# Attention's instruction order comes from a wider search, value sums may wait three tiles, and the last group runs its query blocks in another order

## The chip, the cores and the metric

One core of a Trainium2 chip runs the whole kernel. The metric is the device time of one execution in microseconds (us), as the median of repeated runs.

## What is computed

A cross-attention and a routed feed-forward network, each with a residual. The core of the reference:

```python
qh = (q @ Wq.T + bq).reshape(Bb, Lq, H, hd).transpose(0, 2, 1, 3)      # q = layernorm(x), 4096 x 512, 16 heads of 32
kh = (kv @ Wk.T + bk) ...                                              # kv: 3202 x 512
scores = jnp.einsum('bhqd,bhkd->bhqk', qh, kh) * scale
mask = jnp.arange(Lkv)[None, :] <= jnp.arange(Lq)[:, None]
attn = jax.nn.softmax(jnp.where(mask, scores, -inf), axis=-1)
out = jnp.einsum('bhqk,bhkd->bhqd', attn, vh)
x = x + out @ Wo.T + bo
# feed-forward: x = x + layernorm(W_dec(sigmoid(W_c2s(top-2 of 8 experts(W_s2c(sigmoid(W_enc(layernorm(x)))))))))
```

The attention is causal: a query sees keys up to its own index.

## The kernel before

Four stages follow one another: projections of keys, values and queries (0 to 289 us), attention (289 to 2083 us), the output projection, and the feed-forward network. The change is about attention, and about the order in which the two stages after it go through the rows.

**Tiles.** The 16 heads are taken in 4 groups of 4 heads (`NG`, `HG`). In each group the 4096 queries are 8 blocks of 512 (`QB`, named j = 0 to 7), and the keys are 26 tiles of 128. Block j sees `key_tiles(j)` = 4, 8, 12, 16, 20, 24, 26, 26 key tiles. A step (`ALL_STEPS`) is one group, block and key tile, with four heads. In the last tiles of a block, on the diagonal, only 384, 256 or 128 queries are left.

**Work of a step.** TensorE makes four score matmuls (line 1215, keys by queries) into a ring of three banks, `s_bank`. ScalarE takes the exponentials (line 1046) into one of six slots of `pT`. TensorE weighs the values with them (line 1232), always two steps together, a "pair of tiles". In the program's listing this is 8 matmuls of 512 columns; the profiler records each as two.

**Row maxima.** The softmax maximum is found ahead. For each block TensorE computes the scores a second time, queries by keys (line 1168, one "unit" is 128 queries by up to 512 keys of one head), into a ring of four banks, `m_bank`, and VectorE reduces each (line 1063). When a block's units are done, its maxima are transposed (line 1179) and copied into the rows that scores of that block use.

**Denominators.** The exponentials of a step are summed for the softmax by one of three ways, `adder(j, kt)`: GpSimd adds the tile to `part_sum` (line 986), or a 1 MB DMA issued by GpSimd adds it to one of two `moved_sum` chains (lines 969 and 972), or a matmul against ones takes it from `pT` (line 1200). Block 0 uses a copy on GpSimd (line 984) for its first tile. In the very last block, from key tile 18, VectorE adds instead of GpSimd (line 1113). Two steps into the next block, TensorE sums the parts (lines 1192, 1195, 1200), after it has waited for all adds and both chains.

**A slot of `pT`** is free for step S + 6 when the values of step S have been weighed and its add or transfer is done (`reuse_slot` on ScalarE).

**What sets the order.** Each engine takes its instructions in program order. The order on TensorE is written by a search when the kernel is built (`Orders`). At each point it may place a score, a unit or a pair of values; it holds the states with the least lost TensorE time by its own constants for TensorE, ScalarE and VectorE. Two bounds matter here: a pair of values is forced when 4 scores stand behind its tiles (`VALUES_BEHIND`), and 60 states are kept (`KEPT`). The search knows nothing of the time of GpSimd's adds, of transfers, or of when they free a slot.

Of the kernel before, what the change touches and what calls it, by code (L numbers as in the profile page):

```python
# [9 lines left out]
ALU = mybir.AluOpType  # L10
# [3 lines left out]
P = 128  # L14
# [452 lines left out]
STEPS = [(j, kt) for j in range(QB) for kt in range(key_tiles(j))]  # L467
ST = len(STEPS)
FIRST_STEP = [STEPS.index((j, 0)) for j in range(QB)] + [ST]
ALL_STEPS = [(g, s, j, kt) for g in range(NG) for s, (j, kt) in enumerate(STEPS)]  # L470
assert all(key_tiles(j) % 2 == 0 for j in range(QB))


def query_buffer(g, j):
    return (QB * g + j) % QBUFS


def query_loads(g, j):

    return (QB * g + j) // QBUFS + 1  # L480
# [19 lines left out]
def adder(j, kt):  # L500

    if kt > 4 * j or kt == KT - 1:
        return "matmul"
    return "transfer" if j and kt and kt % 2 == 0 and kt <= key_tiles(j) - 4 else "pool"


def pool_adds(j, kt):

    return adder(j, kt) == "pool" and (kt != 0 or j == 0)
# [23 lines left out]
PO = sum(pool_adds(j, kt) for j, kt in STEPS)  # L533
PO_BEFORE = [sum(pool_adds(j, kt) for j, kt in STEPS[:s]) for s in range(ST + 1)]
TR_BEFORE = [[sum(moves(j, kt, c) for j, kt in STEPS[:s]) for s in range(ST + 1)] for c in range(CHAINS)]
TR = [TR_BEFORE[c][ST] for c in range(CHAINS)]


DEN_AFTER, INVERT, SPREAD, NORMALISE, STORE = 2, 1, 2, 3, 7
SUMS_BEHIND = {ST * g + FIRST_STEP[j + 1] + DEN_AFTER: (g, j) for g in range(NG) for j in range(QB) if (g, j) != (NG - 1, QB - 1)}  # L540

# [16 lines left out]
NU = sum(map(len, UNITS))  # L558
UNITS_BEFORE = [sum(map(len, UNITS[:j])) for j in range(QB + 1)]
# [18 lines left out]
def work_axis():  # L578

    t, at = 0, []  # L580
    for S, (g, s, j, kt) in enumerate(ALL_STEPS):
# [11 lines left out]
def released(at, g, j, c):  # L593
# [1611 lines left out]
```

## Time and profile before

| | us |
|---|---|
| median of 3 runs | 2960.18 (2959.51 to 2963.02) |
| the profiled execution | 2962.7 |
| its span, first to last instruction | 2961.1 |
| TensorE busy | 2870.6 (97%) |
| VectorE busy | 1850.8 (63%) |
| ScalarE busy | 1521.0 (51%) |
| GpSimd busy | 1427.1 (48%) |

The span is the profiled execution less 1.6 us around it. "Busy" of TensorE covers pipelined matmuls, so that 97% is not the share in which it does useful work: what a matmul costs is read from the distance between starts. The mean granted clock of TensorE is 0.98 of full speed.

### The profile page before, as it was taken

The numbers are of one execution on the slowest core, as the hardware profiler recorded it, in microseconds if no ns is written. First come the engines' busy times: TensorE is split into PE (matmuls) and PEld (weight loads), VectorE is DVE, ScalarE is ACT, GpSimd is POOL, SyncE is SP. The second block draws the span as 40 slices with busy tenths as digits, with TensorE's granted clock in tenths as the row PEclk, the third lists the DMA queues.
The fourth block names the chain that finished last, engine by engine and source line by source line (L and its number), as shares of the span: only waits on it lengthen the run. The fifth ranks groups of instructions, "written<-read, shape, count | busy, mean of one in ns | idle before, by whom it ended". The sixth has DMA issues, their size and how long they took to land. (4 is left out here: it accounts for less than half of the span.)

```text
span 2961.1 us, 42860 instructions
## 1 busy us (share of the span) xinstructions
PE 2870.6 (97%) x15944; PEld 1702.9 (58%) x15944; DVE 1850.8 (63%) x3451; ACT 1521.0 (51%) x2896; POOL 1427.1 (48%) x657
## 2 busy tenths in 40 slices
PE   8999999999999999999999999999889999999996
PEld 7877555555555554555554555543675666655664
DVE  4367888886688776688775787851653443344434
ACT  3232455666566666566666566676334433344332
POOL 0000365778565788566788556786841110111110
PEclk9998899999999999999999999999999999999998
DMA  6558456668656778665778555687691111011000
GB/s 236 192 191 248 116 140 150 152 155 194 162 150 149 157 158 200 154 147 140 158 166 203 137 139 119 161 187 177 234 299 54 43 43 40 4 43 43 29 29 15
DMA packets 139750, 408.20 MB, mean 138 GB/s; under 512 B 12672, under 2 KB 29568, under 8 KB 112928
## 3 DMA queue, kind: packets, MB, share of 16 engines
q0 software_dynamic: 32272, 226.77, 32.5%
q1 hardware_dynamic: 102096, 169.34, 19.9%
q10 hardware_dynamic: 5184, 9.44, 1.0%
q8 instruction: 126, 2.06, 0.3%
q14 instruction: 72, 0.59, 0.1%
HBM read 114.59 MB, written 70.78 MB: 63 GB/s over the span
## 5 line engine op out<-in xcount | busy, mean ns | idle before, releaser
L1063 DVE TENSOR_REDUCE row_max<-m_bank 128x1 f32<-128x512 f32 (+4 forms) x2240 | 1253.6, 622 | 267.9 <-PE m_bank L1168 173.1
L1046 ACT ACTIVATE pT<-s_bank 128x512 f32<-128x512 f32 (+5 forms) x2176 | 1086.7, 579 | 648.3 <-PE s_bank L1215 471.5
L986 POOL TENSOR_TENSOR part_sum<-part_sum,pT 128x2048 f32<-128x2048 f32 x192 | 887.8, 4624 | 124.9 <-ACT pT L1046 120.9
L1215 PE MATMUL s_bank<-q_sb,k_sb 104*128 104x512 f32 (+3 forms) x2176 | 839.3, 411 | 12.6 <-ACT pT L1046 8.5
L1168 PE MATMUL m_bank<-k_sb,q_sb 96*128 96x512 f32 (+4 forms) x2240 | 843.0, 410 | 7.5 <-POOL max_terms L958 2.5
L1168 PEld LDWEIGHTS m_bank<-k_sb,q_sb 96*128 96x128 f32 x2240 | 432.5, 196 | 204.9 <-DVE row_max L1063 128.3
L1215 PEld LDWEIGHTS s_bank<-q_sb,k_sb 104*128 104x128 f32 x2176 | 410.5, 192 | 208.8 <-ACT pT L1046 122.5
L1232 PE MATMUL o_bank<-pT,v_sb 128*32 128x512 f32 (+5 forms) x4352 | 498.6, 575 | 0.0
L986 POOL TENSOR_TENSOR part_sum<-pT 128x2048 f32<-128x2048 f32 x28 | 127.7, 4560 | 307.7 <-ACT pT L1046 159.9
L1232 PEld LDWEIGHTS o_bank<-pT,v_sb 128*32 128x32 f32 (+1 forms) x4352 | 113.4, 109 | 229.4 <-ACT pT L1046 115.8
L1640 POOL TENSOR_TENSOR f_var_eps<-f_mean_var,eps 128x4 f32<-128x4 f32 x8 | 1.6, 201 | 484.4 <-DVE f_mean_var L1813 484.4
L1654 ACT ACTIVATE sT<-ring,be_col 128x512 f32<-128x512 f32 x59 | 40.6, 688 | 236.0 <-PE ring L1844 236.0
L972 POOL DMA_DIRECT2D moved_sum<-pT x152 | 137.8, 906 | 28.2 <-ACT pT L1046 17.3
L1090 DVE STREAM_TRANSPOSE den<-m_bank 128x512 f32<-128x512 f32 x32 | 22.9, 716 | 164.5 <-PE m_bank L1200 153.1
L1799 DVE CAST sp_hi<-sp_f 128x512 fp32r<-128x512 f32 x64 | 27.3, 426 | 154.9 <-PE acc L1950 132.3
L1887 PE MATMUL ring<-c_parts,wo_w 64*128 64x512 f32 x768 | 113.6, 416 | 6.0 <-ACT y L1677 3.6
L1844 PE MATMUL ring<-f_x_hi,we_hi 128*128 128x512 f32 x256 | 110.2, 431 | 3.9 <-PEq L1836 3.9
L1950 PE MATMUL acc<-wd_hi,sp_hi 128*128 128x512 f32 x256 | 110.8, 433 | 0.0
L280 POOL TENSOR_TENSOR q_var_eps<-q_mean_var,eps 128x4 f32<-128x4 f32 x8 | 1.6, 199 | 223.0 <-DVE q_mean_var L276 223.0
L1887 PEld LDWEIGHTS ring<-c_parts,wo_w 64*128 64x128 f32 x768 | 68.1, 186 | 62.6 <-ACT raw L1683 23.6
L1844 PE MATMUL ring<-f_x_hi,we_lo 128*128 128x512 f32 x256 | 102.1, 399 | 0.0
L1844 PE MATMUL ring<-f_x_lo,we_hi 128*128 128x512 f32 x256 | 102.1, 399 | 0.0
(195 smaller groups left out, 3479.8 us busy)
## 6 DMA issues: line engine op xcount, KB each, us to landing
moved_sum<-pT POOLq DMA_DIRECT2D x208, 1024.0 KB, 7.4
q_sb<-qT_hi SPq DMA_DIRECT2D x64, 256.0 KB, 5.1
k_sb<-kT_hi SPq DMA_DIRECT2D x48, 256.0 KB, 8.5
x_in<-in_x SPq DMA_DIRECT2D x8, 1024.0 KB, 6.0
qT_hi<-q_hi SPq DMA_DIRECT2D x8, 1024.0 KB, 4.2
qT_lo<-q_lo SPq DMA_DIRECT2D x8, 1024.0 KB, 6.5
q_sb<-qT_lo SPq DMA_DIRECT2D x32, 256.0 KB, 4.6
aT<-o_sb ACTq DMA_DIRECT2D x32, 256.0 KB, 5.2
```

Of the source, the lines that this page charges most:

```text
L972: pool.dma_start(moved_sum[:, c], pT[:, slot(S)], accum_op=ALU.add).then_inc(moved[c], 16)
L986: pool.tensor_tensor(total, pT[:, slot(S - 1), :, q0:] if j and kt == 1 else total, pT[:, slot(S), :, q0:], ALU.add).then_inc(pool_added, 1)
L1046: act.activation(pT[0:rows, slot(S), h, q0:], s_bank[(HG * S + h) % S_RING][0:rows, q0:], ACT.Exp, scale=SCALE).then_inc(exp_done, 1)
L1063: dve.tensor_reduce(row_max[:, j % 2, r, h, c:c + 1], m_bank[p % M_BANKS][:, 0:n], AX_X, ALU.max).then_inc(unit_max, 1)
L1168: mm = pe.matmul(out[:, 0:n], q_sb[query_buffer(g, j)][0:R_MAX, h, r * P:(r + 1) * P], k_sb[0:R_MAX, h, at:at + n], start=True, stop=not m ...
L1215: mm = pe.matmul(out[:, q0:], k_sb[0:R_END, h, at:at + P], q_sb[query_buffer(g, j)][0:R_END, h, q0:], start=True, stop=kt < 4 * j)
L1232: mm = pe.matmul(o_bank[h * HD:(h + 1) * HD, q0:], v_sb[0:rows, kt, h * HD:(h + 1) * HD], pT[0:rows, slot(S), h, q0:], start=kt == 0, stop ...
L1654: act.activation(sT[:, m], src[:, :], ACT.Sigmoid, bias=be_col[:, m:m + 1]).then_inc(ring_free, 1)
L1799: dve.tensor_copy(sp_hi[:, m % 2], sp_f[:, m % 2]).then_inc(sp_hi_ready, 1)
L1844: mm = pe.matmul(dst[:, :], ww[:, c, cols], xx[:, c], start=(c == 0 and k == 0), stop=(c == DC - 1 and k == 2))
L1887: mm = pe.matmul(dst[k][:, :], ww[rows, p, c * P:(c + 1) * P], c_parts[rows, part], start=n == 0, stop=n == 2)
L1950: mm = pe.matmul(acc[k][:, :], a[:, m % 2, rows], ww[:, m], start=(m == 0 and n == 0), stop=(m == FC - 1 and n == 2))
```

## The change

- `VALUES_BEHIND` goes from 4 to 12 scores (three tiles); before a block's denominators it stays 4 (`SUMS_LATE`). `KEPT` goes from 60 to 200.
- The search's state gains GpSimd's time, the ends of the two transfer chains and the time at which each slot comes free (`summed`), with constants for an add, a transfer and the normalising.
- In the last group of heads the blocks are taken as 0, 1, 2, 4, 6, 7, 5, 3 (`LAST_ORDER`). All counters that were worked out from the block's number now go by its place in the order (`NUMBER`, `START`).
- VectorE's adds of the last block (`vector_adds`) are gone; GpSimd or transfers make them. Block 0 takes its first tile by a matmul in place of a copy on GpSimd.
- The output projection and the feed-forward network go through the rows in `LAST_ORDER` too (`block_rows`). The inputs of the output projection are loaded at the start of the last but two and of the last block. GpSimd's part of the feed-forward network is written out for each block, no longer as a loop. `STORE` goes from 7 to 6 steps.

```diff
-STEPS = [(j, kt) for j in range(QB) for kt in range(key_tiles(j))]
...
+LAST_ORDER = (0, 1, 2, 4, 6, 7, 5, 3)
+ORDER = [tuple(range(QB))] * (NG - 1) + [LAST_ORDER]
+BLOCKS = [(g, j) for g in range(NG) for j in ORDER[g]]
...
-    if kt > 4 * j or kt == KT - 1:
+    if j == 0 or kt > 4 * j or kt == KT - 1:
         return "matmul"
-    return "transfer" if j and kt and kt % 2 == 0 and kt <= key_tiles(j) - 4 else "pool"
+    return "transfer" if kt % 2 == 0 and kt and kt <= key_tiles(j) - 4 else "pool"
...
-LAST_ADDS = 18
-
-
-def vector_adds(g, j, kt):
-
-    return (g, j) == (NG - 1, QB - 1) and kt >= LAST_ADDS and pool_adds(j, kt)
...
+T_ADD, T_MOVE_BEGUN, T_MOVE, T_SCALED = 4.75, 1.05, 8.3, 1.3
 T_AHEAD, LATE_COST = 3.0, 0.05
-VALUES_BEHIND, KEPT = 4, 60
+VALUES_BEHIND, SUMS_LATE, KEPT = 12, 4, 200
...
+    def summed(self, x, S, end):
+
+        _, j, kt = ALL_STEPS[S]
+        kind, pool, chains, free = adder(j, kt), x.pool, x.chain_end, 0
+        if kind == "transfer":
+            c = chain(j, kt)
+            pool = max(pool, end, x.sums_end if starts_chain(j, kt) else chains[c]) + T_MOVE_BEGUN
+            free = pool + T_MOVE
+            chains = chains[:c] + (free,) + chains[c + 1:]
+        elif kind == "pool" and kt:
+            pool = free = max(pool, end) + T_ADD
...
-        act = max(x.act, pe + T_TO_READ) + 0.06 + (T_EXP - 0.06) * widths(j, kt)
+        act = max(x.act, pe + T_TO_READ, x.slot_end[0] + T_TO_WRITE if h == 0 else 0) + 0.06 + (T_EXP - 0.06) * widths(j, kt)
...
-        if values_may and x.n >= 2 * HG * (x.v + 1) + VALUES_BEHIND:
+        behind = SUMS_LATE if 2 * (x.v + 1) in SUMS_BEHIND else VALUES_BEHIND
+        if values_may and x.n >= 2 * HG * (x.v + 1) + behind:
             return [self.values(x)]
```

What the search makes of this is seen in the built programs. TensorE in block 7 of the second group, around key tiles 18 to 21, where before stands (s_bank: scores, m_bank: units, o_bank: values):

```order
L1215 MATMUL s_bank<-q_sb,k_sb 128x512 x2
L1232 MATMUL o_bank<-pT,v_sb 32x512 x8
L1215 MATMUL s_bank<-q_sb,k_sb 128x512 x2
L1168 MATMUL m_bank<-k_sb,q_sb 128x512 x2
L1215 MATMUL s_bank<-q_sb,k_sb 128x512
L1168 MATMUL m_bank<-k_sb,q_sb 128x512
L1215 MATMUL s_bank<-q_sb,k_sb 128x512
L1168 MATMUL m_bank<-k_sb,q_sb 128x512
L1215 MATMUL s_bank<-q_sb,k_sb 128x512 x2
L1168 MATMUL m_bank<-k_sb,q_sb 128x512
L1215 MATMUL s_bank<-q_sb,k_sb 128x512
```

and of the change at the same place:

```order
L1247 MATMUL s_bank<-q_sb,k_sb 128x512
L1264 MATMUL o_bank<-pT,v_sb 32x512 x16
L1247 MATMUL s_bank<-q_sb,k_sb 128x512
L1199 MATMUL m_bank<-k_sb,q_sb 128x512
L1247 MATMUL s_bank<-q_sb,k_sb 128x512
L1199 MATMUL m_bank<-k_sb,q_sb 128x512
L1247 MATMUL s_bank<-q_sb,k_sb 128x512 x2
L1199 MATMUL m_bank<-k_sb,q_sb 128x512 x2
```

The values of key tiles 18 to 21 stand together (x16), where each two tiles stood by themselves (x8). Over the whole program 272 pairs stood alone before; now 71 of them stand directly behind another pair, and the stretches of scores and units between values grow: 26 of them had 22 or more jobs before, and 97 have now.

TensorE at the end of attention, before (the last rows of block 7, and the final denominators):

```order
L1215 MATMUL s_bank<-q_sb,k_sb 128x512 x8
L1232 MATMUL o_bank<-pT,v_sb 32x512 x8
L1215 MATMUL s_bank<-q_sb,k_sb 128x512 x8
L1232 MATMUL o_bank<-pT,v_sb 32x512 x8
L1215 MATMUL s_bank<-q_sb,k_sb 128x512 x4
L1232 MATMUL o_bank<-pT,v_sb 32x512 x8
L1192 MATMUL m_bank<-part_sum,ones 32x512 x4
L1195 MATMUL m_bank<-moved_sum,ones 32x512 x8
```

and of the change (block 3, from its key tile 0, after the denominators of block 5):

```order
L1247 MATMUL s_bank<-q_sb,k_sb 128x512 x17
L1264 MATMUL o_bank<-pT,v_sb 32x512 x8
L1247 MATMUL s_bank<-q_sb,k_sb 128x512 x3
L1264 MATMUL o_bank<-pT,v_sb 32x512 x8
L1247 MATMUL s_bank<-q_sb,k_sb 128x512 x3
L1264 MATMUL o_bank<-pT,v_sb 32x512 x8
L1247 MATMUL s_bank<-q_sb,k_sb 128x512 x12
L1264 MATMUL o_bank<-pT,v_sb 32x512 x8
```

The last block has 16 key tiles in place of 26. Behind the last unit stand 97 scores, 73 of them of the full 512 queries, where 137 stood, 133 of them full.

GpSimd at the end of attention, before:

```order
L986 TENSOR_TENSOR part_sum<-part_sum,pT 128x2048
L972 DMA moved_sum<-pT 128x2048
L986 TENSOR_TENSOR part_sum<-part_sum,pT 128x2048
L972 DMA moved_sum<-pT 128x2048 x3
L876 UNCONDITIONAL_BRANCH
```

and of the change:

```order
L997 DMA moved_sum<-pT 128x2048
L1009 TENSOR_TENSOR part_sum<-part_sum,pT 128x2048
L997 DMA moved_sum<-pT 128x2048
L1009 TENSOR_TENSOR part_sum<-part_sum,pT 128x2048
L997 DMA moved_sum<-pT 128x2048
L897 UNCONDITIONAL_BRANCH
```

The last transfer (key tile 12 of 16) now stands behind an add of GpSimd (key tile 11).

## Rows read from the trace of the kernel before

**Rows 1.** Busy time by stage: attention mixed, its end, both later stages

```profile
core 0: us, PE busy (x) PEld busy (x) DVE busy (x) ACT busy (x) POOL busy (x), PEclk, DMA share, GB/s
289.00:1991.00 1702.00, 1690.08 (x10627) 915.34 (x10627) 1292.07 (x2422) 1063.19 (x2132) 1156.37 (x441) 0.99 0.67 156
1991.00:2083.40 92.40, 81.08 (x394) 26.76 (x393) 14.77 (x13) 56.86 (x114) 57.19 (x25) 0.92 0.71 172
2083.40:2961.10 877.70, 831.08 (x3712) 541.83 (x3712) 385.26 (x733) 320.34 (x524) 199.05 (x154) 0.98 0.22 73
```

**Rows 2.** Timeline of TensorE in group 2, block 5 (start us, us, what)

```profile
1410.03 0.41 PE L1168 MATMUL m_bank<-k_sb,q_sb 96*128 96x512 f32 x1
...
1413.56 0.40 PE L1215 MATMUL s_bank<-q_sb,k_sb 104*128 104x512 f32 x1
1413.80 0.40 PE L1168 MATMUL m_bank<-k_sb,q_sb 96*128 96x512 f32 x1
1414.13 1.92 PE L1232 MATMUL o_bank<-pT,v_sb 128*32 128x512 f32 x16
1415.98 0.50 PE L1168 MATMUL m_bank<-k_sb,q_sb 96*128 96x512 f32 x1
1416.32 0.40 PE L1215 MATMUL s_bank<-q_sb,k_sb 104*128 104x512 f32 x1
...
1418.67 0.39 PE L1215 MATMUL s_bank<-q_sb,k_sb 104*128 104x512 f32 x1
1419.06 0.50 PE L1168 MATMUL m_bank<-k_sb,q_sb 96*128 96x512 f32 x1
```

**Rows 3.** Timeline: values with denominators directly behind them

```profile
1998.81 1.92 PE L1232 MATMUL o_bank<-pT,v_sb 128*32 128x512 f32 x16
2000.55 1.04 PE L1192 MATMUL m_bank<-part_sum,ones 128*32 128x512 f32 x8
```

**Rows 4.** Waits of TensorE's weight loads in attention (total us, times, longest)

```profile
PEld m_bank L1168 <- DVE row_max L1063: 125.1, 235, 0.8
PEld s_bank L1215 <- ACT pT L1046: 122.5, 326, 1.8
```

**Rows 5.** Timeline of the end: one pair of tiles without units

```profile
2062.13 0.96 PE L1215 MATMUL s_bank<-q_sb,k_sb 104*128 104x512 f32 x3
2062.75 4.03 ACT L1046 ACTIVATE pT<-s_bank 128x512 f32<-128x512 f32 x8 [1.48 <-PE s_bank L1215]
2063.40 2.45 PE L1215 MATMUL s_bank<-q_sb,k_sb 104*128 104x512 f32 x5 [0.30 <-ACT pT L1046]
2065.78 1.92 PE L1232 MATMUL o_bank<-pT,v_sb 128*32 128x512 f32 x16
2067.64 0.96 PE L1215 MATMUL s_bank<-q_sb,k_sb 104*128 104x512 f32 x3
```

**Rows 6.** Timeline of VectorE and ScalarE beside rows 2

```profile
1410.48 3.68 DVE L1063 TENSOR_REDUCE row_max<-m_bank 128x1 f32<-128x512 f32 x6
1410.23 4.56 ACT L1046 ACTIVATE pT<-s_bank 128x512 f32<-128x512 f32 x9 [5.51 <-PE s_bank L1215]
```

**Rows 7.** Busy time in blocks 6 and 7 of the third group (columns as rows 1)

```profile
1471.60:1551.90 80.30, 80.22 (x500) 43.96 (x499) 60.48 (x121) 54.69 (x107) 65.41 (x25) 1.00 0.72 160
1551.90:1637.00 85.10, 83.17 (x483) 42.05 (x483) 53.95 (x105) 56.34 (x109) 69.48 (x26) 0.98 0.89 205
```

**Rows 8.** Landing of moved_sum transfers: block 6, block 7 (as rows 7), end of attention

```profile
DMA to landing us min/median/max: 4.6/7.4/8.6
DMA to landing us min/median/max: 5.6/11.4/13.7
DMA to landing us min/median/max: 4.6/7.0/10.5
```

**Rows 9.** Waits of ScalarE in attention: for a transfer to free a slot

```profile
ACT pT L1046 <- DMA moved_sum<-pT: 5.4, 6, 1.7
```

**Rows 10.** GpSimd's adds and transfers in attention, by form

```profile
L986 POOL TENSOR_TENSOR part_sum<-part_sum,pT 128x2048 f32<-128x2048 f32 x192 | 887.8, 4624 | 124.9 <-ACT pT L1046 120.9 <-DMA moved_sum<-pT 0.6
L972 POOL DMA_DIRECT2D moved_sum<-pT x152 | 137.8, 906 | 28.2 <-ACT pT L1046 17.3 <-DMA moved_sum<-pT 8.8 <-POOL part_sum L986 1.5
```

More of the change, by code:

```diff
@@ L557 @@
 UNITS = [max_units(j) for j in range(QB)]
-NU = sum(map(len, UNITS))
-UNITS_BEFORE = [sum(map(len, UNITS[:j])) for j in range(QB + 1)]
+UNITS_BEFORE = [sum(len(UNITS[j]) for _, j in BLOCKS[:n]) for n in range(NB + 1)]
 ROWS_BEHIND, ROWS_EARLY = 8, 3
@@ L611, in wanted @@
     jobs = []
[L612 to L620 removed]
+    for n, (g, j) in enumerate(BLOCKS):
+        for i, unit in enumerate(UNITS[j]):
+            if n and i == ROWS_BEHIND:
+                jobs.append((("rows", *BLOCKS[n - 1]), 0, at[max(0, START[n - 1] - ROWS_EARLY)][0]))
+            jobs.append((("unit", g, j, i), released(at, g, j, unit[2]), at[-1][-1]))
+    last = at[START[NB - 1] - ROWS_EARLY][0]
     jobs[-1] = (jobs[-1][0], jobs[-1][1], last - 8)
[L622 removed]
+    jobs.append((("rows", *BLOCKS[NB - 1]), last - 1, last))
     lead = len(UNITS[0]) + ROWS_BEHIND + 1 + ROWS_BEHIND
@@ L710, in score @@
             copied = act + T_TO_WRITE
-        return x._replace(pe=pe, act=act, last="scores", behind_values=behind, n=x.n + 1, copied=copied, order=(x.order, "score"),
+        return x._replace(pe=pe, act=act, pool=pool, chain_end=chains, slot_end=slots, added=added, last="scores", behind_values=behind, n=x.n + 1,
+                          copied=copied, order=(x.order, "score"),
                           exp_end=x.exp_end[1:] + (end,), step_end=x.step_end + ((end,) if h == HG - 1 else ()))
@@ L994, in _ @@
-                for S, (g, s, j, kt) in enumerate(ALL_STEPS):
-                    if adder(j, kt) == "transfer":
-                        move(S, g, s, j, kt)
-                    if pool_adds(j, kt) and not vector_adds(g, j, kt):
-                        add(S, g, s, j, kt)
+                    total = part_sum[:, n % 2, :, q0:]
+                    pool.tensor_tensor(total, pT[:, slot(S - 1), :, q0:] if kt == 1 else total,
+                                       pT[:, slot(S), :, q0:], ALU.add).then_inc(pool_added, 1)
@@ L999, in _ @@
+                for S in range(len(ALL_STEPS), len(ALL_STEPS) + NORMALISE):
                     if S - NORMALISE in SUMS_AT:
@@ L1643, in body @@
                     pool.wait_ge(out_ready, 4 * (b + 1))
[L1644 to L1645 removed]
+                    pool.dma_start(out[block_rows(b), :].rearrange("(t p) n -> p t n", p=P), y[:, :, :]).then_inc(out_stored, 16)
+                for b in range(QB):
+                    body(b)
                 pool.wait_ge(out_stored, 16 * QB)
```

289 lines of the change are left out of this document (152 added, 137 removed).

## The prediction, made before the changed kernel had run

> **What bounds the kernel now.** I read the busy times by stage first, then the starts of TensorE's instructions, then who is waited for, then the slots and transfers. By stage [rows 1], attention takes 1702 + 92 us of 2961, and in its first 1702 us TensorE is busy 1690 us. VectorE is busy 1292 us there, GpSimd 1156, ScalarE 1063. So TensorE bounds attention, and what the change can give is TensorE time that does no work. The stages behind attention (878 us) get the same work in another order of rows, so I cost them at nothing.
>
> "Busy" hides lost time, so the starts must be read. Between the unit at 1410.03 and the unit at 1413.80 lie 16 scores and units, 3.77 us, 0.235 us each [rows 2]. This is the price of a job (a full score or unit) for which nothing is late. Lost time shows in three places.
>
> 1. At values. From the unit at 1413.80 to the score at 1416.32 stand two jobs and one pair of tiles, 2.52 us [rows 2]. Less 2 x 0.235, a pair by itself costs 2.05 us. With the same kind of matmuls directly behind it, a pair takes 2000.55 - 1998.81 = 1.74 us [rows 3]. So entering and leaving a pair costs 0.31 us.
> 2. At jobs that wait for a bank. The unit at 1419.06 starts 0.39 us after its forerunner, 0.155 too late [rows 2]. Weight loads wait 235 times for VectorE and 326 times for ScalarE [rows 4], 561 in all. What reaches TensorE is between 0.10 us each (0.34 - 0.235, a job that starts 0.34 us after its forerunner) and 0.155 us, so 56 to 87 us.
> 3. At the end of attention, where no units are left. A pair of tiles there takes 2067.64 - 2062.13 = 5.51 us [rows 5], while its work costs 8 x 0.235 + 2.05 = 3.93 us. The rest, 1.58 us, is TensorE waiting for exponentials: ScalarE needs 4.03 us for eight and then idles 1.48 us, because only three banks run ahead of it [rows 5]. Per full score that is 0.20 us.
>
> **The change, part by part.** The sum is made against the profiled execution, 2962.7 us (a span of 2961.1 and 1.6 around it). The median of the runs is 2960.2, so 2.5 us come off at the end.
>
> *Pairs of values that stand together.* 71 of 272 pairs now follow another. Each saves 0.31 us: 71 x 0.31 = 22 us. Nothing hides this cost, for it is on TensorE itself.
>
> *A shorter end.* 133 full scores stood behind the last unit, now 73: 60 x 0.20 = 12 us. Narrow scores rise from 4 to 24; I take them as not waiting. If they waited like full ones, 137 against 97 scores would give 8 us, the lower bound. Less waiting also leaves fewer stretches of lower clock; the granted clock is 0.92 over the last 92 us, against 0.99 before [rows 1]. I count 1 us for that, between 0 and 3.
>
> *Waits in the mixed part.* Of the 56 to 87 us, the end holds about 13 x 1.6 = 21. So 35 to 66 us lie in the mixed part, where the search has more freedom (lag 12 in place of 4, 200 states in place of 60). Against it stand longer stretches. A score and a unit take TensorE 0.47 us, and VectorE needs 3.68 / 6 = 0.61 us for the unit [rows 6], so each pair of jobs puts VectorE back by 0.14 us, and ScalarE (4.56 / 9 = 0.51) by 0.04. Four banks take this up for a while: the stretch up to 1413.80 has 18 jobs, of which none behind the second waits [rows 2]. Jobs beyond the eighteenth of their stretch rise from 259 to 1170, 911 more. If VectorE held each of them up at 0.14 / 2 = 0.07 us, it would cost 64 us. I do not take this value: behind two pairs together (3.5 us) VectorE has caught up, and the stretches of 26 have two scores in a row near their end. The bounds are a gain of 35 us (half of the larger figure) and a loss of 64. I take a gain of 8, nearer to the row of 18 jobs without a wait.
>
> *Slots and transfers.* A transferred tile frees its slot after the transfer has landed. In ordinary blocks this takes 7.4 us, 8.6 at most; in block 7 of a group, where the next group's keys and values are loaded too and the DMA engines are 0.89 busy, 11.4 us, and up to 13.7 [rows 7, 8]. Before, this cost 6 waits and 5.4 us [rows 9]. I priced the work that stands between the last score of each transferred tile and the first of step S + 6, at 0.235 a job and the prices of a pair above. In block 7 of the first three groups 2 of 33 such distances were under 13 us; now 14 are, the shortest 10.8. A tile needs about 1.1 us to the end of its exponentials (0.62 until ScalarE starts after a score, and 0.5 for one) [rows 5], 0.2 allowed for the issue and 11.4 to land, 12.7 us. At about 1 us for each short one, less what is paid already, I take a loss of 8 us; 0 if the waits pull the work apart once, 20 if the longest landings are met. Elsewhere 9.9 us at most are needed, and 5 of 206 distances are under 10: nothing.
>
> By the Trainium skill (DMA: Bandwidth & Descriptors, the anatomy of one SWDGE DMA) a DMA takes about 2.0 us plus its bytes at 436 GB/s, an estimate of 4.4 us for 1 MB. The trace disagrees, with medians of 7.4 and 11.4 us. By that rule this loss and the next would both be nothing, the sum 43 us and the time 2917, inside the forecast case; I go by the rows.
>
> *The last denominators.* VectorE's adds are gone, and the last transfer (key tile 12) stands behind GpSimd's add of tile 11. From the end of tile 11's exponentials: an add of 4.62 us [rows 10], and 7.0 to 10.5 to land [rows 8], 11.6 to 15.1 us. TensorE until then has pair 10/11 (2.0), the rest of tiles 12 to 15 at ScalarE's pace (about 5), and two narrower pairs (2.8), near 10 us. It then stands for 1.6 to 5 us; I take 3. Before, the last transfer had landed in time.
>
> *Nothing else.* The removed copy and the adds on VectorE lie on engines with idle time. GpSimd is busy 65 to 69 us in blocks of 80 to 85 [rows 7], so it stays covered if a block shortens by 2 or 3 us; if that cover were gone, each of its adds would show. The chain behind the last matmul (copy, invert, multiply, store, load) is unchanged.
>
> Sum: 22 + 12 + 1 + 8 - 8 - 3 = 32 us. 2962.7 - 32 = 2930.7, and against the median 2928.
>
> **The rivals.**
>
> *VectorE takes it back (slower).* In long stretches TensorE runs at VectorE's pace. For it: 0.61 against 0.47 us [rows 6], and 235 waits on it already [rows 4]. Against it: 18 jobs without a wait [rows 2], and 1292 us busy in 1702 [rows 1]. Without the term of 8, the rest gives 24 us, so it decides from 24 / 0.07 = 340 of the 911 jobs. At all 911 the time is 2962.7 - 24 + 64 - 2.5 = 3000 us; at 500 it is 2971.
>
> *The slots pay for the pairs (no change).* The values wait longer, so slots are held longer. If landings go to 11.4 us in ordinary blocks too, since the same bytes come faster (the DMA share there is 0.72 now), 47 of all 206 distances are under 12 us and 119 under 14. At 0.25 us for each of the 119 it costs 30 us, and the time is 2962.7 - 32 + 30 - 2.5 = 2958. Against it: landings of 8.6 at most in block 6 [rows 8].
>
> By the Trainium skill (the same page, that issuing engines are not separate DMA queues) all DMAs share 16 engines and interleave. The trace agrees, since transfers land later in the stretch with loads (11.4 against 7.4 us).
>
> *The search does more (much faster).* Half of the waits in the mixed part go, 33 us in place of 8, and the slots cost nothing: 2928 - 25 - 8 = 2895.
>
> *The change does nothing.* Values were not held back by the bound of 4. This can be set aside: the built order has the 71 joined pairs, and their price is TensorE's own.
>
> **How the numbers follow.** The forecast case, a gain between 10 and 57 us (2905 to 2950), gets 0.70. The large gain gets 0.10, no change by the slots 0.11, VectorE 0.09. A measurement of this kernel tells 0.2%, about 6 us, from no change. Of the 0.11, 0.06 is within it and 0.05 still faster. Faster is then 0.70 + 0.10 + 0.05 = 0.85, same 0.06, slower 0.09. The range leaves out half of each outer case: from 2893 to 2962. The terms' own bounds for the likeliest case, mixed part between -10 and +30 and slots between 0 and 20, give 2905 to 2950.
>
> **What the profile after would show.** Values in runs of 32 recorded matmuls about 3.5 us long, with the next job 0.1 us behind. The last unit about 70 to 80 us before the end of attention. Waits of weight loads for VectorE and ScalarE fewer than 561, or, if VectorE is the rival, more, in the second half of long stretches. ScalarE waiting for moved_sum some 10 to 20 times, most in block 7 of a group. A gap of a few us before the final denominators. Attention ending near 2050 us, and the same 878 us behind it. I am wrong if joined pairs bring waits of ScalarE or VectorE that weigh as much as their 0.31 us, or if the later stages, in their new order of rows, change by more than 2 us.

## The result, and the profile after

| | before | after |
|---|---|---|
| median of the runs, us | 2960.7 (2959.5 to 2963.0, 4 runs) | 2979.3 (2970.0 to 2985.0, 4 runs) |
| the profiled execution, us | 2962.7 | 2970.0 |
| its mean granted clock | 0.982 | 0.977 |

The ratio is 1.0063, with a 95% interval of 1.0042 to 1.0085. The change makes the kernel 0.6% slower; I had forecast 2928 us, 1.1% faster. The profiled execution is the fastest of the four after; the others ran at a clock of 0.970 to 0.973. Among these four, the time goes with the clock: with "lost" for (1 - clock) x span, each us lost goes with 0.70 us of time. Used on other kernels below, this 0.70 is an estimate from four runs.

By stage, busy times of the changed kernel (columns as [rows 1]; its last unit is at 2005, and the last row is a stretch inside attention):

```profile
289.00:2005.00 1716.00, 1691.66 (x10577) 926.42 (x10577) 1286.14 (x2416) 1056.99 (x2137) 1173.95 (x443) 0.98 0.67 156
2005.00:2082.60 77.60, 73.57 (x437) 29.89 (x439) 3.61 (x10) 47.48 (x103) 52.41 (x21) 0.91 0.71 162
2082.60:2968.30 885.70, 831.35 (x3724) 541.63 (x3716) 389.21 (x738) 322.99 (x528) 200.34 (x155) 0.98 0.21 73
1230.00:1251.00 21.00, 21.00 (x84) 11.94 (x87) 11.89 (x28) 7.32 (x15) 6.33 (x3) 0.51 0.25 98
```

The end behind the last unit is 78 us, as predicted, and the stages behind attention take about what they took. The loss is in the mixed part, whose granted clock was 0.99 [rows 1] and is now 0.98. The fourth row shows how: for 21 us TensorE has half its clock (0.51), though it is busy all the time. I call such a stretch at half clock a dip.

The joined pairs do what they should. TensorE in group 2 (timeline):

```profile
1360.71 0.39 PE L1199 MATMUL m_bank<-k_sb,q_sb 96*128 96x512 f32 x1
1361.03 3.64 PE L1264 MATMUL o_bank<-pT,v_sb 128*32 128x512 f32 x32
1364.60 0.50 PE L1199 MATMUL m_bank<-k_sb,q_sb 96*128 96x512 f32 x1
1364.94 0.39 PE L1247 MATMUL s_bank<-q_sb,k_sb 104*128 104x512 f32 x1
```

From 1360.71 to 1364.94 stand two jobs and two pairs, 4.23 us; less 2 x 0.235, two joined pairs cost 3.76 us, where two lone ones cost 2 x 2.05 = 4.10 [rows 2]. That is 0.34 us for each of the 71.

What came instead is seen first in TensorE's waits (total us, times, longest):

```profile
PEld s_bank L1247 <- ACT pT L1075: 90.1, 312, 1.3
PEld m_bank L1199 <- DVE row_max L1095: 83.4, 224, 0.8
PE s_bank L1247 <- DMA q_sb<-q_sb: 13.2, 6, 3.2
PE m_bank L1224 <- DMA moved_sum<-pT: 2.5, 1, 2.5
```

The first two are [rows 4], fewer than before (536 against 561). The third is new at this size (3.1 us, 3 times before): the first score of a block waits for the DMA that spreads the block's row maxima over the rows of `q_sb`. The timeline of group 3 shows one (SPq is SyncE issuing a DMA):

```profile
1787.79 0.28 PE L1210 MATMUL m_bank<-ident_b,neg_parts 128*104 128x128 bf16 x2
1788.10 0.59 ACT L1047 ACTIVATE q_sb<-m_bank 8x512 fp32r<-8x512 f32 x1 [0.84 <-PE m_bank L1210]
1788.79 0.71 SPq L913 DMA_DIRECT2D q_sb<-q_sb  x1
...
1795.80 0.50 PE L1247 MATMUL s_bank<-q_sb,k_sb 104*128 104x512 f32 x1 [2.76 <-DMA q_sb<-q_sb]
```

The transpose (line 1210) is placed `ROWS_EARLY` = 3 steps ahead of the block. From its start over the copy, the issue and the landing it is 8.0 us to the first score. Three diagonal steps are short, and before they had values between them; now these wait, and TensorE is through with them 2.8 us too early. Before, by my prices, this distance was never under 6.4 us; after, 11 blocks have 4.1 to 5.8. Four of them wait for 2.5 us or more (at 391, 1032, 1481 and 1796), and at each of these four stalls a dip of 3.4 or 6.8 us begins, 23.9 us in all.

Second, the long dip (timeline, its start and its end; lines 1250 and 1202 add the causal mask on the diagonal):

```profile
1228.30 0.51 PE L1199 MATMUL m_bank<-k_sb,q_sb 96*128 96x512 f32 x1 [1.23 <-DVE den L1123]
...
1229.21 0.40 PE L1247 MATMUL s_bank<-q_sb,k_sb 104*128 104x512 f32 x1
1229.47 0.50 PE L1199 MATMUL m_bank<-k_sb,q_sb 96*128 96x512 f32 x1
...
1230.51 0.63 PE L1247 MATMUL s_bank<-q_sb,k_sb 104*128 104x512 f32 x1
1230.93 0.63 PE L1199 MATMUL m_bank<-k_sb,q_sb 96*128 96x512 f32 x1
...
1231.88 0.46 PE L1199 MATMUL m_bank<-k_sb,q_sb 96*128 96x128 f32 x1
1232.14 0.33 PE L1202 MATMUL m_bank<-mask,ident_b 128*128 128x128 bf16 x1
...
1246.21 5.65 PE L1264 MATMUL o_bank<-pT,v_sb 128*32 128x512 f32 x32
1251.80 0.73 PE L1199 MATMUL m_bank<-k_sb,q_sb 96*128 96x512 f32 x2
```

From 1230.5 a full job takes 0.42 us in place of 0.235. Up to 1246.2 stand 58 matmuls: 10 full scores and units, 20 narrow ones (128 to 384 columns) and 28 for the mask. Then the first values in 23 us come. They start at half clock, and the clock is back within them, at 1250.8.

I accounted for attention job by job in both profiled executions, from the first unit (269.5, after 268.3) to the last denominators (2076.8, after 2082.6). Each distance between starts is taken less its usual price; at half clock, half of the time is put down to the clock. The rows for turns and waits depend on my prices:

| us in attention | before | after | difference |
|---|---|---|---|
| entering and leaving values | | | -22.5 |
| small waits, under 0.5 us | 152.6 | 148.6 | -4.0 |
| stalls over 0.5 us | 10.2 | 25.4 | +15.2 |
| gaps inside values and denominators | 2.2 | 3.4 | +1.2 |
| low clock | 30.7 | 47.8 | +17.1 |
| sum; duration 1807.3 to 1814.3 | | | +7.0 |

Both kernels begin attention in a dip, 44.4 us long before and 34.1 after. It is in the row for the clock and makes that row 5 us smaller after. From there to the last values TensorE was at half clock for 13.7 us before and 58.0 after; the half-clock times in attention given below are counted in this way.

### The profile page after: what moved, and what is told of

It is laid out like the page before. It is cut to its first block and busy times, and to the rows that moved or that the text cites. A ratio compares the mean times of both kernels' runs of the same rounds, so it can differ in the third digit from the quotient of the medians.

```text
span 2968.3 us, 42821 instructions
## 1 busy us (share of the span) xinstructions
PE 2862.4 (96%) x15944; PEld 1714.5 (58%) x15944; DVE 1836.5 (62%) x3447; ACT 1508.5 (51%) x2896; POOL 1441.2 (49%) x657
## 5 line engine op out<-in xcount | busy, mean ns | idle before, releaser
L1075 ACT ACTIVATE pT<-s_bank 128x512 f32<-128x512 f32 (+5 forms) x2176 | 1073.7, 585 | 660.7 <-PE s_bank L1247 497.0
L1009 POOL TENSOR_TENSOR part_sum<-part_sum,pT 128x2048 f32<-128x2048 f32 x196 | 927.1, 4730 | 91.7 <-ACT pT L1075 88.7
L1247 PE MATMUL s_bank<-q_sb,k_sb 104*128 104x512 f32 (+3 forms) x2176 | 849.5, 413 | 21.2 <-DMA q_sb<-q_sb 17.0
L1199 PE MATMUL m_bank<-k_sb,q_sb 96*128 96x512 f32 (+4 forms) x2240 | 858.3, 411 | 10.5 <-DVE den L1123 3.9
L1247 PEld LDWEIGHTS s_bank<-q_sb,k_sb 104*128 104x128 f32 x2176 | 417.1, 194 | 192.4 <-ACT pT L1075 90.1
L1264 PE MATMUL o_bank<-pT,v_sb 128*32 128x512 f32 (+3 forms) x4352 | 490.4, 580 | 0.5 <-ACT o_sb L1037 0.5
L1264 PEld LDWEIGHTS o_bank<-pT,v_sb 128*32 128x32 f32 x4352 | 122.2, 111 | 259.0 <-issue 162.8
L997 POOL DMA_DIRECT2D moved_sum<-pT x152 | 150.9, 993 | 30.9 <-DMA moved_sum<-pT 15.4
```

The costliest lines, as they stand in the source:

```text
L997: pool.dma_start(moved_sum[:, c], pT[:, slot(S)], accum_op=ALU.add).then_inc(moved[c], 16)
L1009: pool.tensor_tensor(total, pT[:, slot(S - 1), :, q0:] if kt == 1 else total, pT[:, slot(S), :, q0:], ALU.add).then_inc(pool_added, 1)
L1075: act.activation(pT[0:rows, slot(S), h, q0:], s_bank[(HG * S + h) % S_RING][0:rows, q0:], ACT.Exp, scale=SCALE).then_inc(exp_done, 1)
L1199: mm = pe.matmul(out[:, 0:n], q_sb[query_buffer(g, j)][0:R_MAX, h, r * P:(r + 1) * P], k_sb[0:R_MAX, h, at:at + n], start=True, stop=not m ...
L1247: mm = pe.matmul(out[:, q0:], k_sb[0:R_END, h, at:at + P], q_sb[query_buffer(g, j)][0:R_END, h, q0:], start=True, stop=kt < 4 * j)
L1264: mm = pe.matmul(o_bank[h * HD:(h + 1) * HD, q0:], v_sb[0:rows, kt, h * HD:(h + 1) * HD], pT[0:rows, slot(S), h, q0:], start=kt == 0, stop ...
```

## The experiments

All are timed beside the kernel before, whose median stayed at 2960.2 to 2962.3 with a clock of 0.982. "Joined" and "long" are read from the built order: pairs directly behind a pair, and stretches without values over 8 us at full-clock prices. "Distance" is the shortest from a transpose to its block's first score, by the same prices. Clock and lost are medians over all runs.

| kernel | joined | long | distance | clock | lost | us | ratio (95%) |
|---|---|---|---|---|---|---|---|
| before | 0 | 0 | 6.4 | 0.982 | 53 | 2961 | |
| after | 71 | 17 | 4.1 | 0.973 | 82 | 2979.3 | 1.0042 to 1.0085 |
| e1_rows5 | 67 | 17 | 8.0 | 0.975 | 74 | 2963.1 | 0.9995 to 1.0018 |
| e2_lag4 | 0 | 0 | 6.7 | 0.983 | 50 | 2953.5 | 0.9969 to 0.9987 |
| e3_natural | 73 | 19 | 4.1 | 0.971 | 87 | 2985.3 | 1.0042 to 1.0084 |
| e4_before_rows2 | 0 | 0 | 2.5 | 0.980 | 59 | 2971.1 | 1.0029 to 1.0056 |
| g1_rows5_nojoin | 0 | 7 | 8.0 | 0.975 | 76 | 2973.6 | 1.0023 to 1.0053 |
| g2_rows5_lag8 | 56 | 6 | 8.0 | 0.979 | 64 | 2959.3 | 0.9979 to 1.0000 |
| e5_before_lag12 | 66 | 15 | 4.1 | 0.976 | 73 | 2961.9 | 0.9988 to 1.0015 |
| g4_lag4_natural | 0 | 0 | 6.7 | 0.982 | 53 | 2968.5 | 1.0014 to 1.0031 |
| h1_rows5_halfmax | 67 | 17 | 8.0 | 0.978 | 65 | 2940.7 | 0.9924 to 0.9957 |
| h2_before_halfmax | 0 | 0 | 6.4 | 0.984 | 47 | 2944.1 | 0.9928 to 0.9956 |
| h3_lag4_rows5 | 0 | 1 | 8.2 | 0.978 | 65 | 2971.9 | 1.0021 to 1.0041 |
| h4_rows5_even | 10 | 1 | 8.2 | 0.978 | 65 | 2962.1 | 0.9994 to 1.0014 |
| k1_rows5_halfboth | 67 | 17 | 8.0 | 0.973 | 79 | 2927.9 | 0.9871 to 0.9901 |
| k2_before_halfboth | 0 | 0 | 6.4 | 0.981 | 56 | 2927.3 | 0.9872 to 0.9902 |
| k3_lag4_kept60 | 0 | 0 | 6.4 | 0.981 | 56 | 2957.4 | 0.9970 to 0.9991 |
| k4_lag4_unaware | 0 | 0 | 6.7 | 0.981 | 56 | 2960.9 | 0.9987 to 1.0007 |
| l1_rows4_cap25 | 53 | 0 | 6.6 | 0.979 | 62 | 2952.8 | 0.9961 to 0.9983 |
| l2_rows4 | 67 | 17 | 6.0 | 0.968 | 97 | 2980.3 | 1.0049 to 1.0077 |

**Are late maxima the cause?** e1 sends the maxima of the changed kernel further ahead:

```diff
-ROWS_BEHIND, ROWS_EARLY = 8, 3
+ROWS_BEHIND, ROWS_EARLY = 8, 5
```

> The changed kernel with each block's maxima five steps ahead of the block in place of three; the joined pairs stay (67). Theory A (late maxima): the 15 us of stalls of a block's first score and the stretches of low clock behind them (17 us more than before in the profile) go, near 2950 us, at most 2960. Theory B (VectorE holds up the long stretches): nothing changes, near 2979. Theory C (joined pairs of value matmuls, with 32 columns each, lower the clock by themselves): only the stalls go, near 2965, with the time at half clock in attention still over 40 us.

e4 makes them later in the kernel before (`ROWS_EARLY` 3 to 2):

> The kernel before with each block's maxima two steps ahead in place of three: no joined pairs, but in the first group six distances of 2.5 to 2.8 us, and one of 4.3 at the end. Theory A: each short one stalls TensorE for about 4 us, 25 us, and the clock falls behind some of them (5 to 15 us more): 2985 to 3005. Theories B and C: near 2961, since neither long stretches nor joined pairs are there.

e1 took 16 us off, and the stalls over 0.5 us fell from 25.4 to 8.1 us. Of TensorE's waits for this DMA one is left:

```profile
PE s_bank L1247 <- DMA q_sb<-q_sb: 1.4, 1, 1.4
```

e4 cost 10 us, with one stall of 2.7 us at 1997 and a dip of 13.7 us that begins in it. That is less than half of the 24 to 44 us I had expected, since TensorE's six waits for this DMA came to 8.3 us together (3.1 before). So late maxima do cost, but the clock stayed at 0.975 in e1 (in its profile 44.4 us of the mixed part, 320 to 1985, are at half clock, against 47.8 in the changed kernel), and with 67 joined pairs it is only level with the kernel before.

**What do the values' bound and the order of blocks do?** e2 sets the bound back, e3 the order of blocks, g4 both, and e5 makes the bound's part of the change alone on the kernel before:

```diff
-VALUES_BEHIND, SUMS_LATE, KEPT = 12, 4, 200
+VALUES_BEHIND, SUMS_LATE, KEPT = 4, 4, 200
```

> The changed kernel with values forced after 4 scores as before: no pairs stand together, the end is as short as in the change (92 scores behind the last unit), and the shortest distance from a block's transposed maxima to its first score is that of before (6.7 us by the prices of the rows). Theory A: no stalls, no gain of pairs, the shorter end gives 8 to 12 us: 2950 (2944 to 2957). Theory B and C: the same. If this one is near 2979 too, the cause is in the search's new parts or in the order of blocks, and A to C all fall.

```diff
-LAST_ORDER = (0, 1, 2, 4, 6, 7, 5, 3)
+LAST_ORDER = (0, 1, 2, 3, 4, 5, 6, 7)
```

> The changed kernel with the last group's blocks in their natural order: 120 scores behind the last unit in place of 97, stalls at the same blocks. Each full score at the end costs 0.2 us, so 4 to 6 us slower than the change, 2983 to 2986, by every theory; if it is faster than the change, the new order of blocks costs something that I have not seen.

> The kernel e2_lag4 with the last group's blocks in natural order: only the search's knowledge of GpSimd and slots, its 200 states, and the small edits are left. 135 scores behind the last unit in place of 92. By the price of 0.20 us a score at the end, 8 us slower than e2_lag4 (2953.5): near 2961, so no different from before. If it is near 2954, the order of blocks gives nothing and the search's knowledge gives the 7 us.

```diff
-VALUES_BEHIND, KEPT = 4, 60
+VALUES_BEHIND, SUMS_LATE, KEPT = 12, 4, 60
```

> The kernel before with the later bound on values alone (12 scores, 4 before denominators; 60 states, no knowledge of GpSimd or slots, blocks in their order, end as long as before): 66 joined pairs, 101 stretches with 22 or more jobs, four short distances to a block's maxima. Theories C and D: the clock falls to about 0.972 as in the change, and with no shorter end and slots that are not known to the search it is the slowest, 2980 to 2990. If it is near 2960, the fault is not with the values' waiting.

With the bound at 4, the changed kernel is faster than the kernel before (2953.5), at its clock. The order of blocks is worth 13 us there by the ratios, 15 by the medians (2968.5 without it); small waits fall by 12.5 us (151.2 to 138.7), just what the prediction gave the shorter end. With the bound at 12 it is worth 6 us, between runs that spread by 15 and 25 us. e5 shows the bound alone: it saves its turns (272 to 206 entries into values), and its clock falls from 0.982 to 0.976. Its time is the same as before, not the 2980 or more that I had expected. By my prices the turns give 20 to 22 us and the clock costs 14 (an estimate, 19.3 us more lost at 0.70).

**Is it the joined pairs themselves?** g1 is e1 without them, g2 is e1 with a bound of 8:

```diff
-        out = [self.values(x)] if values_may else []
+        out = [self.values(x)] if values_may and x.last != "values" else []
```

> The kernel e1_rows5 (maxima five steps ahead) whose search may not place a pair of values directly behind another unless it must: 0 joined pairs in place of 67, stretches with 22 or more jobs fall from 97 to 47, values may still wait three tiles. Theory C (joining pairs lowers the clock): the mean granted clock returns from 0.975 to 0.981 or more; the 67 pairs cost 0.31 us each again (21 us) and the clock gives 15 back, near 2968. Theory D (uneven order: long stretches of scores and units at ScalarE's or VectorE's pace, with no values between, lower the clock): the clock rises in part, 0.977 to 0.979. If the clock stays at 0.975, neither.

> The kernel e1_rows5 with values forced after 8 scores in place of 12: 56 joined pairs, 85 stretches with 22 or more jobs (97 in e1_rows5). Theory C: joined pairs fall by a sixth, so the clock hardly moves (0.975 to 0.976), near 2962. Theory D: with a shorter lag the long stretches at the others' pace are shorter, clock 0.977 to 0.980, near 2957.

Not the joining: g1 has none, and its clock is as low as e1's (0.975). It only lost the turns, and 10 us, where their price gives 21. g2 lies between (0.979).

**Is it TensorE waiting for VectorE and ScalarE?** h1 and h2 leave out the second half of the columns in VectorE's maxima, in e1 and in the kernel before; k1 and k2 leave out the first half of the columns in ScalarE's full exponentials as well, so that what they compute is no longer the attention:

```diff
-m_bank[p % M_BANKS][:, 0:n], AX_X, ALU.max
+m_bank[p % M_BANKS][:, 0:min(n, 256)], AX_X, ALU.max
```

> The changed kernel with the maxima sent 5 steps ahead, and VectorE takes each row maximum over the first 256 of its 512 scores only (this part of the computation is changed), so that it needs some 0.35 us a unit in place of 0.61 and can hardly hold up TensorE. The order of instructions is the same. Waits theory (values held back lower the clock because the stretches between them run at VectorE's and ScalarE's pace, so that TensorE has gaps): the clock rises from 0.975 towards 0.983, half-clock time in attention falls from 55 us to under 30, and waits on VectorE go; together 2963 falls by 25 us or more, to 2930 to 2940. Rival (the order itself, or values done in bulk, lowers the clock, whatever the gaps): the clock stays at 0.975, only waits on VectorE go (some 20 to 40 us shared with ScalarE), time 2940 to 2955.

> The control for the run above: the kernel before, with the same cut of VectorE's maxima to 256 of 512 scores. It says what VectorE's waits cost there. Both theories: the clock stays near 0.982, for there is little left to give back, and the waits on VectorE go, 10 to 35 us: 2925 to 2950. If the changed kernel gains at least 10 us more by the same cut than this one, VectorE's pace in the longer stretches is what costs it its clock.

```diff
+                    e0 = max(q0, 256) if S >= 24 else q0
...
-act.activation(pT[0:rows, slot(S), h, q0:], s_bank[(HG * S + h) % S_RING][0:rows, q0:],
+act.activation(pT[0:rows, slot(S), h, e0:], s_bank[(HG * S + h) % S_RING][0:rows, e0:],
```

> As the run that halved VectorE's maxima, but ScalarE too takes only columns 256 to 511 of each full score from block 3 on (the exponentials of the other half are left out), so that neither VectorE nor ScalarE can hold up TensorE; values held back 12 scores, maxima 5 steps ahead. The order is the same as there (2940.7 us, clock 0.978). If gaps between jobs, whoever causes them, lower the clock: 0.985 or more in every run, under 10 us at half clock in attention, and time 2880 to 2905. Rival (values taken in bulk, or their place, lower the clock without any gap): clock 0.976 to 0.980, time 2905 to 2930.

> The control: the kernel before with both cuts (maxima over 256 of 512 scores, exponentials of columns 256 to 511 only from block 3 on). Both theories: clock 0.985 or more, waits gone. With halved maxima alone it took 2944.1; the remaining waits are 137 us in attention by my accounting, of which some 60 are ScalarE's: 2880 to 2920. Pairs that stand alone cost 0.31 us each here, so if turns are all that then tells the two orders apart, this one is 15 to 25 us plus the shorter end slower than the one above; if the clock keeps it level, the turns' gain is eaten without any wait.

My theory that waits for these two engines lower the clock falls. VectorE's work halved gave 22 us to the one and 17 to the other, and raised the clock of e1 from 0.975 to 0.978 only. With ScalarE's halved too, small waits are equally low (104.5 and 106.5 us), those of weight loads for ScalarE are 18.0 and 25.7 us, and the clocks stand apart as before: 0.973 against 0.981. The orders take the same time, 2927.9 and 2927.3. The clock costs k1 some 16 us of its joined pairs' 23 (an estimate: 23.4 us more lost, at 0.70). Where its shorter end goes isn't settled; 7.4 us are one wait of its last denominators for a transfer. Its busy times before, in and behind one stretch at half clock (columns as [rows 1]), and TensorE at its ends (timeline):

```profile
1096.00:1113.00 17.00, 14.36 (x100) 5.50 (x92) 1.68 (x3) 5.83 (x19) 14.14 (x6) 1.00 0.60 168
1113.00:1130.00 17.00, 17.00 (x56) 10.32 (x58) 8.36 (x24) 6.11 (x16) 10.82 (x5) 0.51 0.95 204
1130.00:1147.00 17.00, 17.00 (x109) 9.60 (x105) 8.21 (x20) 8.21 (x22) 12.37 (x7) 0.99 0.92 183
```

```profile
1109.09 0.96 PE L1248 MATMUL s_bank<-q_sb,k_sb 104*128 104x512 f32 x3
1112.69 0.33 PE L1200 MATMUL m_bank<-k_sb,q_sb 96*128 96x128 f32 x1 [2.64 <-DMA k_sb<-kT_lo]
...
1126.94 1.48 PE L1200 MATMUL m_bank<-k_sb,q_sb 96*128 96x512 f32 x3
1128.22 1.05 PE L1248 MATMUL s_bank<-q_sb,k_sb 104*128 104x512 f32 x2
1129.21 4.14 PE L1265 MATMUL o_bank<-pT,v_sb 128*32 128x512 f32 x32
1133.28 0.74 PE L1248 MATMUL s_bank<-q_sb,k_sb 104*128 104x512 f32 x2
```

A stall of 2.6 us stands ahead of it. Then 47 matmuls (24 full and 9 narrow scores and units, 14 for the mask) follow each other without a gap for 16 us, all at half clock, until values come, and within these it ends. The kernel before with the same work left out has values 5.4 us behind the same stall, which is 0.7 us long there. Its rows at the same place of the program never leave the full clock:

```profile
1106.00:1123.00 17.00, 16.91 (x110) 7.19 (x109) 4.66 (x11) 7.53 (x22) 11.45 (x5) 1.00 0.46 118
1123.00:1140.00 17.00, 16.26 (x97) 9.40 (x98) 8.36 (x27) 8.15 (x24) 16.27 (x8) 1.00 0.97 241
```

This gave me a new theory: a dip may start for many reasons (a stall, a slow stretch), but it lasts until values come, and values held back make it long. I looked at all 20 profiled executions for stretches at half clock of 10 us or more in the mixed part (320 to 1985 us). There are 26. In 24 of them the first values come before the end, and the end is 0.6 to 4.6 us behind these values; the other two end 0.4 and 0.7 us before. In the changed kernel the dip at 1230 lasts 20.5 us, since its values come after 15.9; the kernel before has a dip of 3.4 us just at this place (1225), with values 2.0 us later.

The theory is too strong as it stands. The same profiles hold 60 dips under 10 us in this part, and 10 of them end before any values come, 7 of these by 3.7 us or more. One is in the changed kernel, behind the same wait as the dip at 1230 and a group later (timeline, then busy times in it and behind it):

```profile
1675.92 0.50 PE L1199 MATMUL m_bank<-k_sb,q_sb 96*128 96x512 f32 x1 [1.52 <-DVE den L1123]
...
1677.44 0.63 PE L1247 MATMUL s_bank<-q_sb,k_sb 104*128 104x512 f32 x1
...
1681.11 0.40 PE L1247 MATMUL s_bank<-q_sb,k_sb 104*128 104x512 f32 x1
...
1684.77 0.64 PE L1264 MATMUL o_bank<-pT,v_sb 128*32 128x512 f32 x4
```

```profile
1677.50:1680.70 3.20, 3.20 (x10) 1.73 (x9) 3.20 (x8) 2.15 (x4) 1.05 (x1) 0.50 0.54 210
1680.90:1684.70 3.80, 3.80 (x23) 2.28 (x22) 3.80 (x7) 3.63 (x8) 3.80 (x2) 1.00 0.18 69
```

Here full scores and units follow the wait, and the clock is back 3.9 us ahead of the values; at 1230 units of 128 columns and masks follow. And length is not all. All 26 long dips begin in stretches that cross the diagonal, with mask matmuls in them. Of the stretches with 22 to 29 scores and units between two runs of values, 366 lie off the diagonal and no dip begins in them, while 13 begin in the 535 on it, though both kinds last about as long (medians of 6.6 and 6.7 us, less half of what they spend at half clock). Of the stretches over 8 us without denominators in them, 216 lie on the diagonal and 4 off it. So what the narrow scores, units and masks do to the clock, beside the missing values, was not tested by itself.

**Long stretches.** h4 makes the search place values as soon as it may once 20 jobs stand behind the last ones. h3 asks whether e1's 5 steps help e2 as well:

> The changed kernel with the maxima sent 5 steps ahead; values may still wait 12 scores, but the search must place a pair as soon as it may once some 20 jobs stand behind the last one. Joined pairs fall from 67 to 10, stretches of 22 jobs or more from 97 to 5. Uneven-order theory (long stretches, then values in bulk, lower the clock): clock back to 0.982 or more, the turns cost what they did before, time 2950 to 2956. Rival (values that come late lower it, however even the stretches are): clock 0.975 to 0.977, time 2965 to 2972.

> The changed kernel with values bound to 4 scores as before, and the maxima sent 5 steps ahead. With values bound to 4, the shortest distance from the transpose to the first score is 6.7 us already, so the late-maxima theory expects little: 2948 to 2955 against 2953.5 with 3 steps. Rival (the stalls above 0.5 us that are left there, 14 us, are late maxima too): they fall to 8 us and the time to 2945 to 2948.

h3 surprised me, 18 us slower than e2. Sending the maxima 5 steps ahead had changed the order early in the first group: one stretch of 39 jobs, 9.0 us, where e2 has its longest, 33 jobs and 7.7 us. The profile shows a dip of 10.2 us in it, at 333 us, and the clock is 0.978 to 0.980 in all runs. By the lost time (15 us more than e2) this makes some 10 of the 18 us, an estimate. h4 has a stretch of this kind at the same place (37 jobs), and the same clock, where the theory asked for 0.982 or more. It had lost its joined pairs too.

l1 is the test: 4 steps, which leave that place alone, a bound of 12, and a cap: once some 26 jobs stand behind the last values, the next pair is placed as soon as it may. l2 is the same without the cap.

```diff
-        if values_may and x.n >= 2 * HG * (x.v + 1) + behind:
+        if values_may and (x.n >= 2 * HG * (x.v + 1) + behind or x.last != "values" and x.behind_values >= EVEN):
```

> The changed kernel (values may wait 12 scores) with maxima sent 4 steps ahead, and one more rule: once some 26 jobs stand behind the last values, the next pair is placed as soon as it may. 53 pairs stay joined, no stretch of scores and units is longer than 6.3 us at full price (17 of them were over 8 us in the changed kernel, up to 10.0), and the shortest distance from a block's transpose to its first score is 6.6 us. Long-stretch theory (TensorE falls to half clock in stretches over some 8 us without values, and stays there until values come): clock 0.981 or more, half-clock time in attention under 20 us, joined pairs worth 53 x 0.31 = 16 us against the best version so far: 2938 to 2950. Rival (values held back or taken in bulk lower the clock by themselves): clock 0.974 to 0.977, time 2958 to 2970.

> The control for the run above: maxima sent 4 steps ahead, without the rule on stretches. 67 pairs joined, 17 stretches over 8 us, up to 10.0. Long-stretch theory: clock 0.973 to 0.976, time 2960 to 2972, so that the rule alone is worth 15 us or more. Rival: the same clock as the run above, within 0.002, and the same time within 6 us.

The cap is worth 27 us, 2980.3 to 2952.8, and lifts the clock from 0.968 to 0.979, though 53 of 67 pairs are still joined. Half-clock time in attention falls from 95.6 to 51.2 us. It is less than I expected of l1 (0.981 and 2938 to 2950): its profile has three dips of 10 to 14 us left, on the diagonal, in stretches of 23 to 25 scores and units (2 to 5 of them narrow) with 6 to 13 mask matmuls. The same place in both (busy times; in l1 the dip is 10.2 us of the 21, in l2 all 20):

```profile
789.00:810.00 21.00, 19.57 (x112) 11.00 (x104) 11.21 (x24) 9.39 (x19) 11.17 (x6) 0.76 0.29 113
```

```profile
806.00:826.00 20.00, 20.00 (x75) 11.62 (x79) 11.74 (x27) 8.15 (x16) 6.39 (x3) 0.50 0.29 111
```

l2 itself was slower than I had expected of it (at most 2972, a clock of 0.973 to 0.976), and it can't be told from e1 by the table's counts: 67 joined pairs and 17 long stretches in both, one step between them, and yet 0.975 against 0.968 and 17 us. g1 has 7 long stretches and e1's clock. So the cap shows that the length of the stretches matters in this order; how many are long does not give the clock.

**What the search's knowledge and its 200 states are worth**, with the bound at 4: k3 keeps 60 states, k4 has the constants for GpSimd and transfers at 0.

> The changed kernel with values bound to 4 scores, and 60 states kept in the search in place of 200. Its order has the same kind of stretches (24 of 22 jobs or more, against 26). If more states find a better order: 2956 to 2962 against 2953.5 with 200. Rival (orders that differ by nothing the constants see differ by several us on the chip, as 2953.5 and 2971.9 for maxima 3 and 5 steps ahead suggest): anything from 2945 to 2975, with the clock between 0.978 and 0.984 making two thirds of the difference.

> The changed kernel with values bound to 4 scores and the search's constants for GpSimd's adds, the transfers and the normalising set to 0, so that it does not know when a slot comes free. If this knowledge is worth something, waits of ScalarE for a transfer rise above 10 us and the time to 2957 to 2965 against 2953.5. Rival (with values bound to 4 scores slots are no limit, only the order is another): within 2948 to 2957, and the same waits of ScalarE for transfers as before, 5 to 7 us.

Each against the kernel before as timed beside it (2962.3, and 2960.2 for e2), the 200 states are worth 1 to 2 us, which is nothing within the intervals, and the knowledge 5 to 6. In k4 ScalarE waits 8.3 us for transfers in place of 6.8, less than I had said, so these don't come by that wait. As e2 and h3 show, orders that look equal differ by this much, and I don't settle it. Nor is it settled why g4, the rest of the change without its bound and its order of blocks, is 6.8 us slower than the kernel before. Part is TensorE's wait for GpSimd before the last denominators, 2.4 us where it was 0.8, and the later stages are 1.5 us longer.

## Why the prediction was wrong

- *Joined pairs, 22 us.* Right. 0.34 us each by the timeline, 22.5 us in the accounting.
- *The shorter end, 12 us and 1 for the clock.* Right: 13 to 15 us by e2 and g4, at a bound of 4. Of the 1 us for the clock, see below.
- *Waits in the mixed part, +8 us.* Of 12 + 8 = 20 us of small waits, the changed kernel gained 4 by my accounting; e2, at a bound of 4, gained 14. So holding values back cost some 10 us of waits, and this term was -8 rather than +8, inside its bounds (the upper one should have been 33, half of 66, not 35). The rival for it, VectorE, did not come true as I put it: fewer waits for it, not more. The granted clock may move this figure as well: in the dip at 1230 TensorE, at half clock, waits for nobody.
- *Slots and transfers, -8 us.* Perhaps under-sized. ScalarE waited 11 times and 14.9 us for a transfer, and twice, 6.9 us, for an add, against 5.4. That is 16 us more on ScalarE; how much of it reached TensorE was not measured by itself. Landings in block 7 of the third group had a median of 11.9 us [rows 8], and in block 6 of 7.6, so the rival of late landings everywhere is out.
- *The last denominators, -3 us.* Right: 2.5 us.
- *Later stages, nothing.* 885.7 against 884.3 us, each from its last denominators on: right.
- *Not in the sum: the row maxima.* I wrote that the chain behind the last matmul is unchanged, and never priced the chain ahead of a block's first score, though its distance is counted in steps and the change takes the values out of these steps. This is +15 us of stalls, and e1's 16 us.
- *The failed step is the clock.* I counted 1 us of gain for it, between 0 and 3, from the end of attention alone. It cost 17 us in the profiled execution, and an estimated 20 by the runs (28.6 us more lost, at 0.70). I used the price of 0.235 us a job for stretches of 22 to 44 jobs, on the row of 18 jobs without a wait [rows 2], and asked only who might be waited for in them, not whether TensorE keeps its clock. k1 and k2 show that the clock falls without waits for VectorE, and with few for ScalarE; l1 and l2 show that a cap on the stretches brings it back from 0.968 to 0.979. Half of the half-clock time in the mixed part (23.9 of 47.8 us) stands at the four late maxima, so this step and the one above are not apart. What holds the clock down within a dip stays open.

The sum with what was missed: 32 - 15 (maxima) - 20 (clock) - 16 (waits) = -19 us, and the medians say -19 too. That it fits so well is luck: the clock's 20 is an estimate and the waits rest on my prices, and what the slots cost TensorE beyond 8 us was not measured and may lie in the waits. Attention, which I had ending near 2050 us, ended at 2082.6.

By the Trainium skill (DMA: Bandwidth & Descriptors, the anatomy of one SWDGE DMA) landings of 1 MB would take an estimated 4.4 us. The trace after disagrees again, with medians of 7.6 and 11.9 us.

The best versions run are l1 (2952.8) and e2 (2953.5). Both beat the kernel before, by 0.3 and 0.2%, and the changed one by 0.9%. e2 is the change with one number set back, l1 needs two numbers and a rule.

## What to carry to other kernels

A planner that knows each engine's waits can still write an order that costs the clock. When an order saves turns by doing one kind of work in bulk, look at how long the others then run without it, and compare the granted clock of all runs, not of one. A lead that is counted in steps ("three steps ahead") is a time only as long as the steps keep their content; where a change takes work out of them, count the lead again. And between two orders from a search, even 17 us (l2 and e1) need not come from the idea: test an idea on more than one order.

## What the runs showed of the hardware

- TensorE at half clock stayed there through 47 back-to-back matmuls of scores, units and masks, 16 us without a gap (k1), and through 58 in the changed kernel, 15.9 us. In 24 of 26 dips of 10 us or more it was back 0.6 to 4.6 us behind the start of the next values; in 7 of 60 shorter ones it was back 3.7 us or more ahead of the next values. Which property of the work decides this isn't shown. Values contract over 128 rows, with weight loads of 0.11 us for 32 columns; scores and units contract over 104 and 96 rows, with weight loads of 0.19 us for 128.
- No dip began in 1044 stretches of 18 to 34 scores and units off the diagonal, and 53 began in 1346 stretches of 18 or more on it (20 profiled executions, 320 to 1985 us).
- The mean clock differs between runs of the same kernel: the lowest and highest were 0.970 and 0.977 after, 0.966 and 0.978 in e3, 0.975 and 0.985 in h1, whose times lie 26 us apart, while the kernel before stays between 0.978 and 0.986 over all of its runs.
- The whole way of a block's maxima, from the transpose to the first score that may use them, took 8.0 us (1787.79 to 1795.80): 0.3 transpose, 0.6 for the copy of 8x512, 0.7 issue, and most of the rest the DMA on its way.
